# Explicit drains in place of VectorE's own semaphore waits, in a fused mixture-of-experts and gated-scan block

## What is computed

```python
x = x + 0.5 * ffn(layernorm(x))      # 16 experts, 128 -> 256 -> 128, gelu, top 2, comb = renormalised softmax weights
x = x + attn(layernorm(x))           # q,k,v,g and complex a; scan over time a*state + k*v; q*real*silu(g) @ wo
x = x + 0.5 * ffn(layernorm(x))      # the same weights again
```

## Time and profile before

| quantity | value |
|---|---|
| median of 3 runs | 873.49 us (866.84 to 874.31) |
| the profiled execution's own time | 879.9 us |
| its span in the profile | 878.2 us |
| mean granted TensorE clock | 0.866 |
| VectorE busy | 535.2 us, 61% |
| TensorE matmul busy | 705.5 us, 80% |

### The profile page before, as it was taken

One profiled execution on the slowest core, in us unless ns is written; L12 is line 12 of the kernel. 1 busy time (PEld: TensorE's weight loads), 2 busy tenths in 40 slices (PEclk: granted clock), 3 DMA queues, 4 the chain that ended last, 5 costly groups with the idle time before them and its releaser, 6 DMA issues.

```text
span 878.2 us, 15790 instructions
## 1 busy us (share of the span) xinstructions
PE 705.5 (80%) x4409; PEld 586.2 (67%) x4410; DVE 535.2 (61%) x1281; ACT 513.4 (58%) x1064; POOL 600.7 (68%) x551
## 2 busy tenths in 40 slices
PE   4667998998876998886978769986798888999880
PEld 4253988885366993486953669933688778888770
DVE  5896200218679977599974799674879469010311
ACT  1211567666777647777567776477567345666450
POOL 3377560777888867768867647677587777777575
PEclk9755799999968898988989688987698978999995
DMA  9897699894147661446833176541295865989882
GB/s 327 302 374 219 180 276 258 250 274 134 39 121 223 196 179 58 117 126 180 258 107 100 50 200 188 179 129 45 61 268 162 251 174 166 277 251 284 280 263 89
DMA packets 189278, 167.13 MB, mean 190 GB/s; under 512 B 19024, under 2 KB 176528, under 8 KB 188304
## 3 DMA queue, kind: packets, MB, share of 16 engines
q1 hardware_dynamic: 121168, 106.83, 40.7%
q0 software_dynamic: 16384, 33.72, 12.9%
q10 hardware_dynamic: 51648, 25.63, 9.9%
HBM read 104.57 MB, written 61.51 MB: 189 GB/s over the span
## 4 chain that ended last, share of the span: by engine, by line
PE 54%; ACT 15%; DVE 10%; DMA 10%; issue 5%; POOL 3%; SPq 2%; ACTq 0%; POOLq 0%; DVEq 0%
PE bank L793 17%; PE bank L810 15%; PE bank L870 8%; DMA WUP<-up_weights 7%; PE bank L783 4%; PE bank L719 4%; PE bank L882 3%; POOL got L493 2%; ACT eo L546 2%; PE bank L709 2%; DVE stats L922 1%; ACT kv L508 1%; DVE XL L977 1%; ACT XT L588 1%; SPq L366 1%
## 5 line engine op out<-in xcount | busy, mean ns | idle before, releaser
L493 POOL DMA_INDIRECT got<-rows_out,IDX x256 | 286.8, 1120 | 126.7 <-issue 71.8
L793 PE MATMUL bank<-xsT,WUP 128*128 128x128 f32 x1564 | 228.0, 292 | 47.7 <-ACT xsT L557 34.0
L793 PEld LDWEIGHTS bank<-xsT,WUP 128*128 128x128 f32 x1564 | 206.4, 205 | 56.5 <-issue 41.3
L472 POOL DMA_INDIRECT rows_in<-XL,IDX x128 | 159.2, 1244 | 85.0 <-DVE IDX L1037 33.9
L810 PE MATMUL bank<-W,hidT 128*128 x1564 | 214.1, 280 | 3.5 <-ACT hidT L538 1.5
L810 PEld LDWEIGHTS bank<-W,hidT 128*128 128x128 f32 x1564 | 194.2, 195 | 9.0 <-issue 6.1
L480 POOL DMA_INDIRECT rows_in<-XL,IDX x128 | 141.9, 1109 | 55.5 <-issue 25.7
L538 ACT ACTIVATE hidT<-bank 128x512 f32<-128x512 f32 x200 | 117.6, 588 | 86.4 <-PE bank L793 85.9
L546 ACT ACTIVATE eo<-bank,xs 128x128 f32<-128x128 f32 x391 | 122.7, 364 | 68.2 <-PE bank L810 61.5
L870 PE MATMUL bank<-XT,WA 128*128 128x512 f32 x192 | 96.4, 664 | 17.8 <-DVE qg L1087 10.4
L557 ACT ACTIVATE xsT<-bank 128x256 f32<-128x256 f32 x200 | 73.3, 373 | 49.6 <-PE bank L783 47.9
(11 more groups left out here) (144 smaller groups left out, 863.2 us busy)
## 6 DMA issues: line engine op xcount, KB each, us to landing
WUP<-up_weights SPq DMA_DIRECT2D x400, 128.0 KB
xs<-rows_in SPq DMA_DIRECT2D x100, 258.0 KB, 4.8
rows_out<-eo ACTq DMA_DIRECT2D x91, 256.0 KB
rows_in<-kv SPq DMA_DIRECT2D x16, 774.0 KB, 12.2
rows_in<-XL,IDX POOLq DMA_INDIRECT x256, 3.4
got<-rows_out,IDX POOLq DMA_INDIRECT x256
out<-X SPq DMA_DIRECT2D x4, 1024.0 KB, 5.3
X<-in_L_attn_x SPq DMA_DIRECT2D x3, 1024.0 KB, 11.3
```

Source lines behind the costliest of these rows:

```text
L472: pool.indirect_dma_start(rows_in[slot], bass.IndirectOffsetOnAxis(IDX[:, g, j, 0:1], 0), XL[:, b, j, :], None).then_inc(first_put[i], 16)
L493: pool.indirect_dma_start(got[:, k, j, :], None, rows_out[SLOT[f, g, half]][0:rows, :], bass.IndirectOffsetOnAxis(IDX[:, g, j, k:k + 1], 0 ...
L793: ins = pe.matmul(ps[2 + u % 2][:, k * P:(k + 1) * P], WUP[:, u, a, c * P:(c + 1) * P], xsT[:, u % 2, a * P:(a + 1) * P], start=True, stop ...
```

## The change

Every wait of VectorE on a semaphore that it raised itself, and that stood there for its own next operation, gives place to an explicit `dve.drain()`. The semaphore `dve_chain`, its 433 increments and the function `link` are gone. The operations, their order, their operands and the other engines' programs are the same. The semaphores that other engines wait for are still raised where they were. Ahead of the last product of `scan` two drains stand one behind the other. The wait for `xl_ready` in `weigh` stays. The core of the diff:

```diff
@@ measure, norm
-                link(ins)
+                dve.drain()
@@
                 for _ in range(3):
-                    link(dve.tensor_tensor(na[:, c], rs[:, c], rs[:, c], mult))
-                    link(dve.scalar_tensor_tensor(out=na[:, c], in0=na[:, c], scalar=-0.5, in1=var[:, c], op0=mult, op1=mult))
-                    link(dve.scalar_tensor_tensor(out=rs[:, c], in0=na[:, c], scalar=1.5, in1=rs[:, c], op0=add, op1=mult))
+                    dve.tensor_tensor(na[:, c], rs[:, c], rs[:, c], mult)
+                    dve.drain()
+                    dve.scalar_tensor_tensor(out=na[:, c], in0=na[:, c], scalar=-0.5, in1=var[:, c], op0=mult, op1=mult)
+                    dve.drain()
+                    dve.scalar_tensor_tensor(out=rs[:, c], in0=na[:, c], scalar=1.5, in1=rs[:, c], op0=add, op1=mult)
+                    dve.drain()
...
                 ins.then_inc(norm_ready, 1)
-                dve.wait_ge(norm_ready, n + 1)
+                dve.drain()
@@ rank
                 ins.then_inc(rank_read, 1)
-                dve.wait_ge(rank_read, n + 1)
-                link(dve.tensor_tensor(sel, hot, pos.unsqueeze(1).broadcast_to([P, 2, T, E]), mult))
-                link(dve.tensor_reduce(rowf[:].rearrange("p t k -> p k t").unsqueeze(3), sel, AX.X, add))
+                dve.drain()
+                dve.tensor_tensor(sel, hot, pos.unsqueeze(1).broadcast_to([P, 2, T, E]), mult)
+                dve.drain()
+                dve.tensor_reduce(rowf[:].rearrange("p t k -> p k t").unsqueeze(3), sel, AX.X, add)
+                dve.drain()
@@ combine
-                    link(dve.tensor_tensor(xq, got[:, 0, 4 * q:4 * q + 4, :], xq, add))
+                    dve.tensor_tensor(xq, got[:, 0, 4 * q:4 * q + 4, :], xq, add)
+                    dve.drain()
                     dve.tensor_tensor(xq, got[:, 1, 4 * q:4 * q + 4, :], xq, add).then_inc(combined, 1)
-                dve.wait_ge(combined, 4 * n + hi)
+                dve.drain()
@@ scan
-                link(dve.tensor_tensor(XT[:], XT[:], tmp[3], add))
-                dve.wait_ge(proj_dve, 8 * (n + 1))
+                dve.tensor_tensor(XT[:], XT[:], tmp[3], add)
+                dve.drain()
+                dve.drain()
                 dve.tensor_tensor(kv[:], XT[:], qg[:], mult).then_inc(y_ready, 1)
```

More of the change, by code:

```diff
@@ L281, in build @@
         comb_ready, ct_ps, ct_sb, bias_ps, biased = sem("comb_ready"), sem("ct_ps"), sem("ct_sb"), sem("bias_ps"), sem("biased")
-        dve_chain, pool_chain = sem("dve_chain"), sem("pool_chain")
+        pool_chain = sem("pool_chain")
         rank_read, x_added, gs_ready = sem("rank_read"), sem("x_added"), sem("gs_ready")
@@ L910, in _ @@
         def _(dve):
[L911 to L916, removed]
             def measure(g, col, arriving=False):
@@ L936, in norm @@
                 dve.tensor_tensor(var[:, c], stats[:, c, 2], stats[:, c, 5], add)
-                link(dve.tensor_tensor(m2[:, c], stats[:, c, 1], stats[:, c, 4], add))
+                dve.tensor_tensor(m2[:, c], stats[:, c, 1], stats[:, c, 4], add)
+                dve.drain()
                 if router is not None:
@@ L991, in route @@
                                   BR[:].unsqueeze(1).broadcast_to([P, T, E]), add).then_inc(logits_read, 1)
-                dve.wait_ge(logits_read, n + 1)
+                dve.drain()
                 for j in range(T):
                     ins = dve.max(MX[:, j, :], LG[:, j, :])
-                link(ins)
+                dve.drain()
                 dve.tensor_tensor(gap[:], MX[:, :, 1], MX[:, :, 0], sub).then_inc(gap_ready, 1)
                 best = MX[:, :, 0:2].rearrange("p t k -> p k t").unsqueeze(3).broadcast_to([P, 2, T, E])
-                link(dve.tensor_tensor(hot, LG.unsqueeze(1).broadcast_to([P, 2, T, E]), best, ALU.is_equal))
+                dve.tensor_tensor(hot, LG.unsqueeze(1).broadcast_to([P, 2, T, E]), best, ALU.is_equal)
+                dve.drain()
                 for k in range(2):
                     if k == 1:
[L1001 to L1005, removed]
+                        dve.tensor_tensor(hot[:, 1, :, :], hot[:, 1, :, :], hot[:, 0, :, :], ALU.is_gt)
+                        dve.drain()
+                    dve.tensor_tensor_scan(nth, keep[:].rearrange("p e t -> p (e t)"),
+                                           marks[:, k, :, :].rearrange("p t e -> p (t e)"), 0.0, mult, add)
+                    dve.drain()
+                    dve.scalar_tensor_tensor(out=hot[:, k, :, :], in0=nth.rearrange("p (t e) -> p t e", t=T)[:, :, 0:E],
+                                             scalar=1.0, in1=hot[:, k, :, :], op0=ALU.is_equal, op1=mult)
+                    dve.drain()
                 dve.tensor_tensor(mask[:], hot[:, 0, :, :], hot[:, 1, :, :], add).then_inc(mask_ready, 1)
@@ L1017, in rank @@
                     dve.tensor_scalar(WGT[:, g, 1, :], share[:], 0.5, None, mult)
-                link(dve.memset(off[:] if tiles < T else off[:, :, 0:1], 0.0))
+                dve.memset(off[:] if tiles < T else off[:, :, 0:1], 0.0)
+                dve.drain()
                 dve.wait_ge(rank_ps, kind_no[("R", f, g)] + 1)
                 counts = ps[5][:, T * E:2 * T * E].rearrange("p (t e) -> p e t", t=T)
-                link(dve.tensor_copy(off[:, :, 1 + mine.start:1 + mine.stop], counts[:, :, mine]))
@@ L1022, in rank @@
[L1022 to L1027, removed]
@@ L1028, in rank @@
-                link(dve.tensor_tensor(basee[:], cum[:], nte[:], sub))
-                link(dve.scalar_tensor_tensor(out=off[:, :, 0:T], in0=basee[:].unsqueeze(2).broadcast_to([P, E, T]),
-                                              scalar=float(P), in1=off[:, :, 0:T], op0=mult, op1=add))
+                dve.tensor_copy(off[:, :, 1 + mine.start:1 + mine.stop], counts[:, :, mine])
+                dve.drain()
+                dve.tensor_tensor_scan(off[:].rearrange("p e t -> p (e t)"), keep[:].rearrange("p e t -> p (e t)"),
+                                       off[:].rearrange("p e t -> p (e t)"), 0.0, mult, add)
@@ new lines, in rank @@
+                dve.drain()
+                dve.tensor_scalar(nte[:], off[:, :, T:T + 1].rearrange("p e o -> p (e o)"), 1.0 / P, 127.0 / 256.0, mult, add)
+                dve.drain()
+                dve.tensor_scalar(nte[:], nte[:], 12582912.0, -12582912.0, add, add)
+                dve.drain()
+                dve.tensor_tensor_scan(cum[:], onesf[:, 0:E], nte[:], 0.0, mult, add)
+                dve.drain()
+                dve.tensor_tensor(basee[:], cum[:], nte[:], sub)
+                dve.drain()
@@ L1031, in rank @@
+                dve.scalar_tensor_tensor(out=off[:, :, 0:T], in0=basee[:].unsqueeze(2).broadcast_to([P, E, T]),
+                                         scalar=float(P), in1=off[:, :, 0:T], op0=mult, op1=add)
+                dve.drain()
                 ins = dve.tensor_tensor(pos[:], ps[5][:, 0:T * E].rearrange("p (t e) -> p t e", t=T),
@@ L1051, in weigh @@
                 dve.scalar_tensor_tensor(out=xg, in0=xl, scalar=LIFT, in1=xg, op0=sub, op1=add)
-                link(dve.tensor_tensor(hot, hot, WGT[:, g, :, :].unsqueeze(3).broadcast_to([P, 2, T, E]), mult))
+                dve.tensor_tensor(hot, hot, WGT[:, g, :, :].unsqueeze(3).broadcast_to([P, 2, T, E]), mult)
+                dve.drain()
                 dve.tensor_tensor(LG[:], hot[:, 0, :, :], hot[:, 1, :, :], add).then_inc(comb_ready, 1)
@@ L1059, in add_bias @@
                     dve.tensor_tensor(xq, ps[5 - i][:], xq, add).then_inc(biased, 1)
-                dve.wait_ge(biased, 2 * m + 2)
+                dve.drain()
             def combine(n, g, lo, hi):
@@ L1090, in gate @@
                 dve.wait_ge(inv_ready, n + 1)
-                link(dve.tensor_tensor(tmp[3], tmp[3], tmp[0], mult))
-                link(dve.scalar_tensor_tensor(out=tmp[0], in0=tmp[3], scalar=2.0, in1=tmp[0], op0=sub, op1=mult))
+                dve.tensor_tensor(tmp[3], tmp[3], tmp[0], mult)
+                dve.drain()
+                dve.scalar_tensor_tensor(out=tmp[0], in0=tmp[3], scalar=2.0, in1=tmp[0], op0=sub, op1=mult)
+                dve.drain()
                 dve.tensor_tensor(ci[:], ci[:], tmp[0], mult).then_inc(t_ready, 1)
@@ L1102, in phase @@
                     ins = dve.tensor_scalar(steps16[0], steps16[1], -2.0, corner, mult, add)
-                link(ins)
-                link(dve.scalar_tensor_tensor(out=XT[:], in0=cr[:], scalar=0.0, in1=XT[:], op0=ALU.is_lt, op1=mult))
+                dve.drain()
+                dve.scalar_tensor_tensor(out=XT[:], in0=cr[:], scalar=0.0, in1=XT[:], op0=ALU.is_lt, op1=mult)
+                dve.drain()
                 run = C * T
@@ L1108, in phase @@
                     ins = dve.tensor_tensor_scan(tmp[0][:, at], tmp[3][:, at], XT[:, at], 0.0, add, add)
-                link(ins)
-                link(dve.tensor_scalar(XT[:], tmp[0], 1.0 / PI, ROUND, mult, add))
-                link(dve.tensor_scalar(XT[:], XT[:], ROUND, -PI, sub, mult))
```

(10 more changed lines are left out.)

29 lines of the change are left out of this document (18 added, 11 removed).

## The result

The change made the kernel slower by 0.8%: 880.79 us median of 11 runs (874.94 to 884.17) against 872.41 us of 11 runs of before on the same chips (866.84 to 876.12), a ratio of 1.0078 with a 95% interval of 1.0054 to 1.0102. That ratio is 6.8 us; the medians are 8.4 us apart. The profiled execution took 884.17 us, its span is 882.5 us; it is the slowest of the 11.

A forecast was written before the change was run, and what follows sets the result against it. The prediction took TensorE as busiest (80%), its matmuls holding 54% of the chain, VectorE 10%. It added 120 seams x 0.06 us = 7.2 us to the 873.5 us median: 880.7 us, 0.8% slower, range 869 to 893 us.

The forecast's parts named there:

- The term for the seams: VectorE's seams on the chain: 120 counted in full, each 0.06 us longer with a drain, 7.2 us in all.
- What a drain waits for: At each VectorE seam: the drain sees the end of the operation ahead of it 0.035 us late.
- The drain's own time: At each VectorE seam: the drain itself takes 0.017 us, read from VectorE's drain at the program's end.
- From the drain to the next start: At each VectorE seam: 0.04 us from the sequencer's last own instruction to the next operation's start.
- The count of seams: VectorE's code: 502 seams, 124 on the chain, 88 of those before 82 us; 120 count in full.
- The cover: Middle of the kernel: slack of 1.5 us behind a gate and 6 us behind a scan hides seams off the chain.
- The early release: Rival at VectorE's seams: a drain ends before the producer does, 0.12 us start to start, 862.7 us, faster; chance 0.08.
- No change in price: Rival at VectorE's seams: only 0.02 us more a seam, 2.4 us in total, 875.9 us; chance 0.27.
- The head's delay: Rival from 80 to 200 us: half of the head's 5.3 us is returned as transfers go on, 878.1 us; chance 0.15.
- The dear drain: Rival at VectorE's seams: 0.16 us more each, 892.7 us; chance 0.18, shared with torn cover, 888.3 us.

The follow-up runs named there:

- the two repetitions: The changed kernel timed again against the kernel before, in two later comparisons: 881.64 us, ratio 1.0076, and 880.93 us, ratio 1.0063.
- the met wait: Kernel before with a wait met since the start added behind each own wait, which stays with the consumer; no drains: 874.95 us against 875.39, ratio 0.999.
- the drains off the chain alone: Kernel before with drains only where its chain of work did not run, 367 of 502, semaphores elsewhere: 875.9 us against 876.6, ratio 0.9989.
- the head alone: Kernel before with drains only in the stages ahead of the third route: 879.46 us against 875.39, ratio 1.005; on the slow chip 1003.33 us, ratio 1.0015.
- the drains on the chain alone: Kernel before with drains only in the head, the stages from 199 to 214 us and two late routes: 879.03 us, ratio 1.0025; repeated 882.0 us, ratio 1.0047.
- the rest alone: Kernel before with drains only from the third route on: 877.15 us against 875.39, ratio 1.0032; on the slow chip 1004.39 us, ratio 1.0032.
- the sequencer's wait: Kernel before with a met wait ahead of each own wait, making the own wait a sequencer instruction; no drains: 1010.9 us against 1001.9, ratio 1.011.

## Why the prediction was right

The time was forecast at 880.7 us and measured at 880.79 us. The direction and the mechanism were right: a drain lengthens each seam between dependent operations, and only the seams on the chain of work count. The closeness of the time is luck in three ways. The base, 873.5 us from 3 runs, was 1.1 us above the median of 11. The term for the seams was too high, 7.2 us where the measured price gives 4.9. And pauses were left out. The change itself is only known to a few us: 8.4 us by the medians and 6.8 us by the ratio at first, 6.7 and 5.5 us in the two repetitions.

- **What a drain waits for.** The step took 0.035 us from the operation's end to the drain's end. The chain shows 0.03 us.
- **The drain's own time.** The step added 0.017 us for it, from the drain on an idle engine. This was the mis-sized term: the drain has already begun while the operation runs (the 36 drains behind L950 have a median duration of 181 ns, from shortly after the operation's start), so only its end counts. Without it the sum would have been 0.075 us a seam, which is what was measured.
- **From the drain to the next start.** 0.04 us forecast, 0.04 us measured. The price of a seam was thus 0.041 us instead of 0.06 us, and the term for 120 seams 4.9 us instead of 7.2 us.
- **The count of seams** on the chain, 124, and its head, 88: the head was 4.05 us late where 5.3 us were forecast, and 3.6 us is the count at the measured price. VectorE was busy 60.34 of the first 80 us against 64.02 before, so its idle time there grew by 3.7 us, not by 5. The parts of the head moved by their share: from the first to the last small operation of a norm, 13 seams or 0.53 us, the second norm took 0.50 us longer and the third 0.59 (0.9 us was forecast, for 15 or 16 seams); the second route, with 8 seams or 0.33 us, took 0.33 us longer.
- **What was left out.** Seven pauses of 0.4 us. The ordinary seam of 0.075 us is inside each, so a pause adds some 0.3 us, and the two in the head some 0.6 us. On chips of normal speed pauses of 0.4 us come only with drains: the eight traces with drains have 40 of them, each at such a number; with the met wait, at the same number of instructions, two of 0.26 us are left, and before has none at its own such numbers. What they are stays open. The expectations call them fetches of instructions, and places that repeat every 128 instructions fit that; but no packet of the instruction queues (q8 and q14 of the page) was under way during any of the seven in the trace after, so the transfer itself was not what held VectorE.
- **The cover.** Confirmed by the drains off the chain alone (0.9989) and by the 5.6 us behind the scan and 2.6 us behind the gate.
- **The rivals.** The early release would have shown a start-to-start time under 0.21 us; it is 0.25 us. No change in price would have been 0.02 us a seam; 0.041 us lies halfway between that and the forecast's 0.06, so the seam's price alone does not favour the forecast over this rival. The head's delay was not given back, by the timings of the head alone. The dear drain would have been over 0.35 us.

What stays open: at 4.9 to 5.1 us for the chain and some 0.6 us for the head's pauses, the sum is about 5.6 us. The three comparisons of the change gave 5.5 to 6.8 us by their ratios, and 5.6 us lies inside the interval of each. So nothing is left that asks for another cause, but a further cause worth 1 us would not be seen. The parts are less well measured: the drains on the chain alone gave 2.2 and 4.1 us, less than the head alone, which they contain (4.4 us), the rest alone 2.8 us, the drains off the chain about -1 us. Whether on-chain and off-chain drains together cost more than each alone can't be told at intervals of 0.3%.

## What to carry to other kernels

Of the three forms tried here, a dependence between two small operations of VectorE is cheapest as a semaphore whose wait rides on the consumer (0.033 us); a drain costs 0.075 us, a wait in an instruction of its own 0.10 us, most likely because the sequencer hands over the next operation only after the release. Where an operation needs two waits, issue the one that is released last first, so that it stays with the operation: the order alone was worth 0.07 us a seam here. Count such seams only along the chain of work: 367 of the 502 cost nothing that could be measured.

## What the runs showed of the hardware

- VectorE's sequencer runs ahead: 458 more instructions than before cost nothing when none of them carried a late release (874.95 us against 875.39). The changed kernel has 457 more: 502 drains, less waits that had been instructions of their own, as at the earlier trace rows.
- A second drain on the idle engine lengthens the seam by 0.045 us, of which the drain itself is 0.02 us.
- With drains VectorE pauses for 0.4 us in front of some of its instructions whose number is 64 more than a multiple of 128: 40 pauses in eight traces, and none that long without a visible cause at another number.
- A wait of the sequencer's own costs more than a drain at the same place, 0.28 against 0.25 us from start to start.
- On one chip the kernel before took 1001.9 us and the four others 1003 to 1017 us. There VectorE's seams were far longer for a while, whether by drain or by semaphore. VectorE's timeline with the head's drains, then with the sequencer's wait:

```profile
76.53 0.17 DVE L963 SCALAR_TENSOR_TENSOR steps<-steps 128x16 f32<-128x16 f32 x1 [1.22 <-issue]
```

```profile
79.99 0.18 DVE L960 SCALAR_TENSOR_TENSOR rs<-steps,rs 128x16 f32<-128x16 f32 x1 [1.23 <-DVE steps L959]
```

The operations last 0.17 us as always, and the seams 1.2 us. It isn't known what held them, and no trace of the kernel before was taken on this chip; a chip like this hides a change of this size.
